# Recommendation ranker on one core: SyncE fetches one field of thirteen tiles, ScalarE another field of seven, GpSimd gathers 396 columns

## The chip, the core and the metric

The kernel runs on one core of a Trainium2 chip. TensorE (PE) multiplies, VectorE (DVE) and ScalarE (ACT) work on tiles in on-chip memory, GpSimd (POOL) issues the gathers from the embedding table, SyncE (SP) issues plain transfers. Each engine has its own instruction queue and waits on semaphores for the others. ScalarE has a queue of its own for issuing transfers, too: what stands in it is issued between its arithmetic instructions, in program order.

The metric is the device time of one execution in microseconds (us), as a median over runs.

## What is computed

A DCN ranker over 2048 rows of 26 ids. An id picks a 64-wide row of an embedding table; the 26 rows of an example make x0, 1664 wide.

```python
x0 = emb[ids].reshape(2048, 26 * 64)              # emb: 125000 x 64, float32
x = x0
for i in range(3):                                # cross layers
    x = x0 * (x @ cross_w[i])[:, None] + cross_b[i] + x
h = relu(x0 @ w1 + b1)                            # 1664 -> 1024
h = relu(h @ w2 + b2)                             # 1024 -> 512
h = relu(h @ w3 + b3)                             # 512 -> 256
y = sigmoid(concat([x, h], 1) @ out_w + out_b)
```

An id at or past the end of the table takes the table's last row.

## The kernel before

The 2048 rows are cut into 16 tiles (t = 0 to 15) of 128 rows, one row per partition. For each tile the 26 fields (f = 0 to 25) of 64 columns are brought into `x_buf[t % 2]`; two neighbouring fields make one chunk k of 128 columns, 13 chunks in all. The chunks go in four groups of 4, 3, 4 and 2 chunks (g = 0 to 3; fields 0 to 7, 8 to 13, 14 to 21, 22 to 25). In tile 15 the groups are cut finer and put in another order: chunks 0-3, 4-6, 7-8, 12, 9-10, 11 (`LAST_GROUPS`).

The way of a group through the engines, per tile: the fields land; DVE replaces rows of ids past the end (`make_whole`, line 516) and counts `x_whole`; PE transposes the chunks into a PSUM bank (`transpose_x`, line 729); ACT copies the bank to `xT_hi` (`x_hi`, line 400); DVE makes the remainder `xT_lo` (`x_lo`, line 523); PE multiplies by the first layer's weights in three passes (`l1`, line 717). After group 3 PE transposes the first layer's result (`transpose_h1`, line 771), once per tile, then runs the third layer of the tile before and the second layer of this tile inside the next tile's beginning. The order of each engine's queue is written out by hand (`begin`, `step`, `last_step`), tile after tile.

Most fields are brought by POOL: one indirect transfer gathers one field of one tile, 128 rows of 256 bytes (line 347). POOL goes through tiles and fields in order. In front of some fields it waits so as not to run too far ahead: at f = 16, from tile 2 on, for the transposition of group 0 of the same tile (line 320), among others.

The rest is fetched row by row, with one plain transfer of 256 bytes for each of 128 rows, whose table addresses come from `at_bytes`:

- SP fetches field `SP_FIELD` of the tiles in `SP_TILES` (lines 287 to 296). For a quarter of a tile it loads 32 addresses into registers (line 292) and issues 32 transfers (line 295), into one of four row buffers; from its fifth tile on it waits until the buffer has been emptied (line 289). SP has nothing else to do in that time.
- ACT fetches field `ACT_FIELD` of `ACT_TILES`, 64 rows per step in shares of 8, 12, 4, 16, 12 and 12 between its other work (`fetch`, line 377), into two row buffers. It does so in every step from tile 1 to tile 14.

In step t, right after `x_hi(t, 2)`, ACT copies the landed rows of SP's and of its own buffer into `x_buf` (`sp_place`, line 369; `act_place`, line 391), if the tile is in the list; `make_whole(t, 3)` waits for both. `of_pool` (line 67) tells which fields are left to POOL.

Of the kernel before, what the change touches and what calls it, by code (L numbers as in the profile page):

```python
# [5 lines left out]
def dcn_ranker_kernel(nc, r_ids, emb, cross_w, cross_b, w1, b1, w2, b2, w3, b3, out_w, out_b, out):  # L6
# [8 lines left out]
    B, F = r_ids.shape  # L15
# [4 lines left out]
    TILES = B // P  # L20
# [15 lines left out]
    def groups(t):  # L36
# [7 lines left out]
    LOW_BITS = 2 ** (H.bit_length() - 1) - 1  # L44

    SP_TILES = [2, 4, 6, 8, 9, 10, 12, 14, 15]
    SP_REGS = 32
    SP_FIELD = F - 2
    SP_BUFS = 4  # L50
# [2 lines left out]

    ACT_TILES = [3, 5, 7, 9, 11, 13, 15]
    ACT_FIELD = F - 1
    ACT_BUFS = 2
    ACT_SHARES = [8, 12, 4, 16, 12, 12]
    assert ACT_FIELD // FPK in GROUPS[-1] and all(
        sum(ACT_SHARES) * (t - 1) >= P * (j + 1) for j, t in enumerate(ACT_TILES)) and P % sum(ACT_SHARES) == 0  # L60
# [6 lines left out]
    def of_pool(t, f):  # L67
        return not (t in SP_TILES and f == SP_FIELD or t in ACT_TILES and f == ACT_FIELD)

# [37 lines left out]
    with ctx:  # L107
        def sb(name, shape, dt=F32):
            return ctx.enter_context(nc.sbuf_tensor(name, shape, dt))
# [4 lines left out]
        def sem(name):  # L114
            return ctx.enter_context(nc.semaphore(name))
# [32 lines left out]

        ONE_BY_ONE = len(SP_TILES) + len(ACT_TILES)
        assert (SP_BUFS + ACT_BUFS) * E + ONE_BY_ONE <= TILES * F  # L150
# [1 line left out]
        act_rows = [ids[:, (SP_BUFS + j) * E:(SP_BUFS + j + 1) * E].bitcast(F32) for j in range(ACT_BUFS)]  # L152
        sp_cols = ids[:, (SP_BUFS + ACT_BUFS) * E:(SP_BUFS + ACT_BUFS) * E + ONE_BY_ONE].bitcast(F32)
        at_bytes = sb("at_bytes", [ONE_BY_ONE, P], I32)
        at_row = {t: i for i, t in enumerate([t for t in SP_TILES if t % 2 == 0] + [t for t in SP_TILES if t % 2])}

        VR = (2 * CROSS + 1) * K1
        vec_rows = sb("vec_rows", [VR, P])
# [86 lines left out]
        sp_cols_ready = sem("sp_cols_ready")  # L245
# [31 lines left out]
        def _(sync):  # L277
# [8 lines left out]
            sync.wait_ge(sp_idx_ready, 1)  # L286
            for i, t in enumerate(SP_TILES):
                if i >= SP_BUFS:
# [61 lines left out]
        def _(act):  # L350
# [18 lines left out]
            def sp_place(t):  # L369
                i = SP_TILES.index(t)  # L370
                act.wait_ge(sp_landed[i % SP_BUFS], 16 * P * (i // SP_BUFS + 1))
                act.activation(x_buf[t % 2][:, SP_FIELD * E:(SP_FIELD + 1) * E], sp_rows[i % SP_BUFS],
                               ACT.Copy).then_inc(sp_placed, 1)
# [3 lines left out]
            def fetch(share):  # L377

                j, p = fetched[0] // P, fetched[0] % P
                if p == 0 and j >= ACT_BUFS:  # L380
                    act.wait_ge(act_placed, j - ACT_BUFS + 1)
                row = len(SP_TILES) + j
                regs = [act.alloc_register(f"act_row{j}_{p + i}") for i in range(share)]
# [7 lines left out]
            def act_place(t):  # L391
                j = ACT_TILES.index(t)
                act.wait_ge(act_landed[j % ACT_BUFS], 16 * P * (j // ACT_BUFS + 1))
                act.activation(x_buf[t % 2][:, ACT_FIELD * E:(ACT_FIELD + 1) * E], act_rows[j % ACT_BUFS],
                               ACT.Copy).then_inc(act_placed, 1)
# [90 lines left out]
        def _(dve):  # L486
# [8 lines left out]
            def split_lo(n):  # L495
                raw, _, lo = parts(n)
                for i in range(2):
                    dve.wait_ge(hi_staged, 2 * n + i + 1)
                    half = half_of(raw, i)
                    dve.tensor_tensor(half_of(lo, i), half, like(bank_of(n, i)[0], half),  # L500
                                      ALU.subtract).then_inc(weights_split, 1)

            def make_whole(t, g):
# [8 lines left out]
                if t in SP_TILES and SP_FIELD in range(a, a + n):  # L512
                    dve.wait_ge(sp_placed, SP_TILES.index(t) + 1)
                if t in ACT_TILES and ACT_FIELD in range(a, a + n):
                    dve.wait_ge(act_placed, ACT_TILES.index(t) + 1)
# [174 lines left out]
            link(dve.tensor_scalar(past[:, 0:QUICK], ids[:, 0:QUICK], float(H), None, ALU.is_ge))  # L690
            dve.wait_ge(idx_ready, 3)
            copied = 0
            for field, tiles in ((SP_FIELD, [t for t in SP_TILES if t % 2 == 0]), (SP_FIELD, [t for t in SP_TILES if t % 2]),
                                 (ACT_FIELD, ACT_TILES)):
                every = tiles[1] - tiles[0]
                assert tiles == list(range(tiles[0], tiles[-1] + 1, every))
                a, b = (t * F + field for t in (tiles[0], tiles[-1]))
                dve.scalar_tensor_tensor(out=sp_cols[:, copied:copied + len(tiles)], in0=past[:, a:b + 1:every * F], scalar=float(H),
                                         in1=idx[:, a:b + 1:every * F], op0=ALU.mult, op1=ALU.add).then_inc(sp_cols_ready, 1)
                copied += len(tiles)  # L700
# [11 lines left out]
        def _(pe):  # L712
# [195 lines left out]
            pe.transpose(h_bank[0][:, 0:VR], vec_rows[:, :], identity[0:VR, 0:VR]).then_inc(vecs_transposed, 1)  # L908
            pe.wait_ge(cross_ready, 1)

            pe.wait_ge(sp_cols_ready, 3)
            pe.transpose(x_bank[1][0:ONE_BY_ONE, 0:P], sp_cols, identity[:, :]).then_inc(sp_cols_transposed, 1)
            pe.wait_ge(sp_idx_ready, 1)
            pe.wait_ge(identity_r_set, 1)
# [30 lines left out]
```

## Time and profile before

| | |
|---|---|
| time, median of 3 runs | 529.95 us (529.79 to 530.59) |
| the profiled execution's own time | 530.56 us |
| its span (first to last instruction) | 528.8 us |
| PE busy in the span | 480.8 us (91%) |
| POOL busy in the span | 379.6 us (72%) |
| DVE, ACT busy | 186.4 us (35%), 84.7 us (16%) |
| granted TensorE clock | full (2.4 GHz) in all 40 slices |
| POOL gathers | 400, mean 0.947 us |
| single-row transfers of SP, of ACT | 1152 (9 tiles), 896 (7 tiles) |

The busy time of POOL counts the gathers only, not the 0.30 us between two of them, in which it is not free for anything else. Transfers that SP and ACT issue do not count as busy time of these engines. A tile lasts some 31 us; the first step, with the loading of the weights, ends near 53 us, and after tile 15's first layer near 516 us only the last layers are left.

### The profile page before, as it was taken

What the parts mean: (1) busy time and instruction counts of PE and PEld (TensorE: products, weight loads), DVE (VectorE), ACT (ScalarE), POOL (GpSimd) and SP (SyncE); (2) the same over time, 40 slices, a digit from 0 to 9 for tenths busy, and PEclk for the clock granted to TensorE, in tenths of its full rate; (3) what the DMA queues carried; (4) which work ended last, traced back from release to release, by engine and by line L of the source; (5) the groups of instructions that cost most, each with busy time, mean ns of one, the idle gap of its engine ahead of it and who ended that gap; (6) DMA issues with size and microseconds to landing.
All of it is one profiled execution on the core that took longest, in us unless ns stands there. A gap on an engine that the chain in (4) does not pass through costs nothing.

```text
span 528.8 us, 11324 instructions
## 1 busy us (share of the span) xinstructions
PE 480.8 (91%) x2912; PEld 442.2 (84%) x2912; DVE 186.4 (35%) x391; ACT 84.7 (16%) x159; POOL 379.6 (72%) x407
## 2 busy tenths in 40 slices
PE   2699899899999989899898989999899898999997
PEld 1399698898989889798887988888898888989996
DVE  5766414232142423224242321424232142423325
ACT  4642111111011111102011110101111010101111
POOL 5777776777777777777777777777777777777720
PEclk9999999999999999999999999999999999999999
DMA  7971111111111111111111111111111111111100
GB/s 234 387 263 29 28 29 27 28 29 27 29 29 29 28 28 30 29 29 29 27 29 26 30 27 30 26 30 29 26 30 25 30 27 28 27 28 28 28 10 2
DMA packets 19700, 24.90 MB, mean 47 GB/s; under 512 B 9305, under 2 KB 10292, under 8 KB 19636
## 3 DMA queue, kind: packets, MB, share of 16 engines
q0 software_dynamic: 12800, 13.13, 11.2%
q1 hardware_dynamic: 4770, 10.74, 5.7%
q10 hardware_dynamic: 2066, 0.31, 0.3%
q8 instruction: 23, 0.38, 0.3%
q14 instruction: 41, 0.34, 0.2%
HBM read 24.41 MB, written 0.01 MB: 46 GB/s over the span
## 4 chain that ended last, share of the span: by engine, by line
PE 55%; POOL 14%; issue 10%; ACTq 9%; DMA 5%; DVE 4%; ACT 3%; POOLq 0%; DVEq 0%
PE l_bank L717 41%; POOL x_raw L347 14%; ACTq L387 8%; DMA x_raw<-in_L_rec_emb,idx 4%; PE x_bank L717 4%; PE x_bank L729 4%; PE h_bank L771 3%; ACT xT_hi L400 2%; DVE x_raw L516 2%; ACTq L384 1%; PE l_bank L802 1%; DVE xT_lo L523 1%; PE h_bank L741 1%; DVE h2T_lo L528 1%; ACT h2T_hi L411 1%
## 5 line engine op out<-in xcount | busy, mean ns | idle before, releaser
L347 POOL DMA_INDIRECT x_raw<-in_L_rec_emb,idx x400 | 378.8, 947 | 125.5 <-issue 107.7
L717 PE MATMUL l_bank<-w_hi,xT_hi 128*128 128x342 f32 (+1 forms) x624 | 144.9, 333 | 3.5 <-DVE xT_lo L523 3.3
L717 PE MATMUL l_bank<-w_lo,xT_hi 128*128 128x342 f32 (+1 forms) x624 | 137.9, 321 | 0.0
L717 PE MATMUL l_bank<-w_hi,xT_lo 128*128 128x342 f32 (+1 forms) x624 | 137.7, 321 | 0.0
L717 PEld LDWEIGHTS l_bank<-w_hi,xT_hi 128*128 128x128 f32 x624 | 104.0, 191 | 7.9 <-DVE xT_lo L523 5.6
L717 PEld LDWEIGHTS l_bank<-w_lo,xT_hi 128*128 128x128 f32 x624 | 106.8, 191 | 0.0
L717 PEld LDWEIGHTS l_bank<-w_hi,xT_lo 128*128 128x128 f32 x624 | 106.3, 190 | 0.0
L523 DVE TENSOR_TENSOR xT_lo<-x_bank,xT_hi 128x512 fp32r<-128x512 f32 (+1 forms) x66 | 38.2, 578 | 158.5 <-ACT xT_hi L400 158.5
L400 ACT ACTIVATE xT_hi<-x_bank 128x512 fp32r<-128x512 f32 (+1 forms) x66 | 33.5, 507 | 270.3 <-PE x_bank L729 220.4
L729 PE MATMUL x_bank<-identity,x_raw 128*128 128x128 f32 x208 | 34.7, 279 | 27.0 <-DVE x_raw L516 27.0
L729 PEld LDWEIGHTS x_bank<-identity,x_raw 128*128 128x128 f32 x208 | 25.0, 142 | 36.7 <-issue 31.0
L516 DVE COPY_PREDICATED x_raw<-past,x_bank 128x512 f32<-128x512 int32 (+1 forms) x66 | 39.9, 605 | 42.7 <-DMA x_raw<-in_L_rec_emb,idx 42.7
L717 PE MATMUL l_bank<-w_hi,h1T_hi 128*128 128x512 f32 x120 | 48.7, 406 | 0.9 <-DVE h1T_lo L528 0.9
L717 PE MATMUL l_bank<-w_hi,h1T_lo 128*128 128x512 f32 x120 | 47.4, 395 | 0.0
L717 PE MATMUL l_bank<-w_lo,h1T_hi 128*128 128x512 f32 x120 | 47.2, 393 | 0.0
L535 DVE TENSOR_TENSOR h<-l_bank,b_rows 128x344 f32<-128x344 f32 (+2 forms) x48 | 23.2, 513 | 49.4 <-PE l_bank L717 49.4
L406 ACT ACTIVATE h1T_hi<-h_bank 128x512 fp32r<-128x512 f32 x30 | 17.6, 598 | 82.1 <-PE h_bank L771 82.1
L717 PEld LDWEIGHTS l_bank<-w_hi,h1T_lo 128*128 128x128 f32 x120 | 22.5, 188 | 5.3
L717 PEld LDWEIGHTS l_bank<-w_hi,h1T_hi 128*128 128x128 f32 x120 | 22.6, 188 | 5.0 <-DVE h1T_lo L528 1.1
L717 PEld LDWEIGHTS l_bank<-w_lo,h1T_hi 128*128 128x128 f32 x120 | 22.6, 189 | 4.1
L528 DVE SCALAR_TENSOR_TENSOR h2T_lo<-h_bank,h2T_hi 128x512 fp32r<-128x512 f32 (+1 forms) x16 | 10.8, 675 | 36.6 <-ACT h2T_hi L411 35.0
L528 DVE SCALAR_TENSOR_TENSOR h1T_lo<-h_bank,h1T_hi 128x512 fp32r<-128x512 f32 (+1 forms) x32 | 20.2, 670 | 9.8 <-ACT h1T_hi L406 9.7
(94 smaller groups left out, 296.5 us busy)
## 6 DMA issues: line engine op xcount, KB each, us to landing
ids<-in_L_rec_emb SPq DMA_DIRECT2D x1152, 0.2 KB
ids<-in_L_rec_emb ACTq DMA_DIRECT2D x896, 0.2 KB
w_raw<-in_L_rec_w SPq DMA_DIRECT2D x18, 512.0 KB, 15.0
x_raw<-in_L_rec_emb,idx POOLq DMA_INDIRECT x400, 2.4
b_rows<-in_L_rec_b SPq DMA_DIRECT2D x1, 512.0 KB
b_rows<-in_L_rec_b SPq DMA_DIRECT2D x1, 256.0 KB
ids<-in_r_ids SPq DMA_DIRECT2D x1, 208.0 KB, 2.7
b_rows<-in_L_rec_b SPq DMA_DIRECT2D x1, 128.0 KB
```

The source lines that it names most:

```text
L347: pool.indirect_dma_start(out=dst, out_offset=None, in_=emb, in_offset=rows).then_inc(landed, 16)
L384: act.load(regs, at_bytes[row:row + 1, p:p + share])
L387: act.dma_start(act_rows[j % ACT_BUFS][p + i:p + i + 1, :].bitcast(U8), emb_bytes[:, bass.DynSlice(at, ROW)], bounds_check="skip_entire_dm ...
L400: act.activation(xT_hi[:, ks[0]:ks[-1] + 1, :].rearrange("p k b -> p (k b)"), x_bank[g % 2][:, 0:len(ks) * P], ACT.Copy).then_inc(xT_hi_re ...
L406: act.activation(h1T_hi[:, half * HB:(half + 1) * HB, :].rearrange("p k b -> p (k b)"), h_bank[half][:, 0:HB * P], ACT.Relu).then_inc(h1T_ ...
L516: dve.copy_predicated(x_buf[t % 2][:, a * E:(a + n) * E].rearrange("p (f e) -> p f e", e=E), past[:, t * F + a:t * F + a + n].rearrange("p ...
L523: dve.tensor_tensor(xT_lo[:, ks[0]:ks[-1] + 1, :].rearrange("p k b -> p (k b)"), x_bank[g % 2][:, 0:len(ks) * P], xT_hi[:, ks[0]:ks[-1] + ...
L528: dve.scalar_tensor_tensor(out=lo, in0=bank[:, 0:cols], scalar=0.0, in1=hi.bitcast(F32), op0=ALU.max, op1=ALU.subtract).then_inc(done, 1)
L535: dve.tensor_tensor(h1[:, a:e], bank[:, 0:e - a], b1_rows[:, a:e], ALU.add).then_inc(h1_ready, 1)
L717: done = pe.matmul(bank[:, 0:b - a], x[:, k, :], w[:, k, a:b], start=(k == 0 and n == 0), stop=(k == last_k and n == 2))
L729: done = pe.transpose(x_bank[g % 2][:, i * P:(i + 1) * P], x_buf[t % 2][:, k * P:(k + 1) * P], identity[:, :])
L771: done = pe.transpose(bank[:, i * P:(i + 1) * P], h1[:, k * P:(k + 1) * P], identity[:, :])
```

## The change

Three numbers change. `SP_TILES` was nine tiles, `[2, 4, 6, 8, 9, 10, 12, 14, 15]`, and becomes the thirteen tiles 2 to 14; `SP_FIELD` stays 24. `ACT_FIELD` goes from 25 to 23, for the same seven odd tiles 3 to 15. POOL gathers what is left: 416 - 13 - 7 = 396 columns, where it was 400.

| tile | POOL's gathers before | after |
|---|---|---|
| 0, 1 | 26 | 26 |
| 2, 4, 6, 8, 10, 12, 14 | 25 | 25 |
| 3, 5, 7, 11, 13 | 25 | 24 |
| 9 | 24 | 24 |
| 15 | 24 | 25 |

The rest follows from that: since the tiles of SP are now one run with step 1, DVE picks SP's addresses in one instruction, not in two, and TensorE waits for two of them, not three.

```diff
-    SP_TILES = [2, 4, 6, 8, 9, 10, 12, 14, 15]
+    SP_TILES = list(range(2, TILES - 1))
...
-    ACT_FIELD = F - 1
+    ACT_FIELD = F - 3
...
-        at_row = {t: i for i, t in enumerate([t for t in SP_TILES if t % 2 == 0] + [t for t in SP_TILES if t % 2])}
+        at_row = {t: i for i, t in enumerate(SP_TILES)}
...
-            for field, tiles in ((SP_FIELD, [t for t in SP_TILES if t % 2 == 0]), (SP_FIELD, [t for t in SP_TILES if t % 2]),
-                                 (ACT_FIELD, ACT_TILES)):
+            for field, tiles in ((SP_FIELD, SP_TILES), (ACT_FIELD, ACT_TILES)):
...
-            pe.wait_ge(sp_cols_ready, 3)
+            pe.wait_ge(sp_cols_ready, 2)
```

POOL's queue at the end of tile 3, before: fields 20, 21, 22, then 23 and 24 in one row, then field 0 of tile 4.

```order
L347 DMA x_raw<-in_L_rec_emb,idx 128x64 [waits chunk_done]
L347 DMA x_raw<-in_L_rec_emb,idx 128x64
L347 DMA x_raw<-in_L_rec_emb,idx 128x64 [waits l2_done,chunk_done,x_transposed]
L347 DMA x_raw<-in_L_rec_emb,idx 128x64 x2
L347 DMA x_raw<-in_L_rec_emb,idx 128x64 [waits chunk_done,x_transposed]
```

The same place after: of fields 23, 24 and 25 only 25 is POOL's.

```order
L347 DMA x_raw<-in_L_rec_emb,idx 128x64 [waits chunk_done]
L347 DMA x_raw<-in_L_rec_emb,idx 128x64
L347 DMA x_raw<-in_L_rec_emb,idx 128x64 [waits l2_done,chunk_done,x_transposed]
L347 DMA x_raw<-in_L_rec_emb,idx 128x64
L347 DMA x_raw<-in_L_rec_emb,idx 128x64 [waits chunk_done,x_transposed]
```

One gather less stands between field 22 of an odd tile and the next tile's first.

DVE's queue in tile 15, groups 2 to 5 of `LAST_GROUPS`, before (`gathered_last` tells of POOL's landings, `act_placed` and `sp_placed` of ACT's copies):

```order
L516 COPY_PREDICATED x_raw<-past,x_bank 128x256 [waits gathered_last2]
L523 TENSOR_TENSOR xT_lo<-x_bank,xT_hi 128x256 [waits xT_hi_ready]
L516 COPY_PREDICATED x_raw<-past,x_bank 128x128 [waits act_placed,sp_placed]
L523 TENSOR_TENSOR xT_lo<-x_bank,xT_hi 128x128 [waits xT_hi_ready]
L516 COPY_PREDICATED x_raw<-past,x_bank 128x256 [waits gathered_last4]
L523 TENSOR_TENSOR xT_lo<-x_bank,xT_hi 128x256 [waits xT_hi_ready]
L516 COPY_PREDICATED x_raw<-past,x_bank 128x128 [waits gathered_last5]
```

And after:

```order
L516 COPY_PREDICATED x_raw<-past,x_bank 128x256 [waits gathered_last2]
L523 TENSOR_TENSOR xT_lo<-x_bank,xT_hi 128x256 [waits xT_hi_ready]
L516 COPY_PREDICATED x_raw<-past,x_bank 128x128 [waits gathered_last3]
L523 TENSOR_TENSOR xT_lo<-x_bank,xT_hi 128x128 [waits xT_hi_ready]
L516 COPY_PREDICATED x_raw<-past,x_bank 128x256 [waits gathered_last4]
L523 TENSOR_TENSOR xT_lo<-x_bank,xT_hi 128x256 [waits xT_hi_ready]
L516 COPY_PREDICATED x_raw<-past,x_bank 128x128 [waits act_placed,gathered_last5]
```

In the last tile chunk 12 (fields 24 and 25) comes from two POOL gathers now, which stand ahead of those of fields 18 to 21, and chunk 11 waits for ACT's copy as well.

## Rows read from the trace of the kernel before

**Rows 1.** Costliest groups: count, busy us, mean ns, idle us before them and its releaser

```profile
L347 POOL DMA_INDIRECT x_raw<-in_L_rec_emb,idx x400 | 378.8, 947 | 125.5 <-issue 107.7
L729 PE MATMUL x_bank<-identity,x_raw 128*128 128x128 f32 x208 | 34.7, 279 | 27.0 <-DVE x_raw L516 27.0
```

**Rows 2.** Chain that ended last (start us, us, what): `transpose_h1` of tiles 1, 2, 3, 5, 13, 14

```profile
84.05 1.15 PE h_bank L771 x8
114.71 1.15 PE h_bank L771 x8
145.24 1.15 PE h_bank L771 x8
...
206.37 1.15 PE h_bank L771 x8
...
455.35 1.15 PE h_bank L771 x8
486.04 1.15 PE h_bank L771 x8
```

**Rows 3.** Timeline (start us, us, what, idle before), tile 13: fields 20 and 21, `make_whole`, transposition of group 2

```profile
438.56 0.94 POOL L347 DMA_INDIRECT x_raw<-in_L_rec_emb,idx  x1 [0.30 <-issue]
439.81 0.94 POOL L347 DMA_INDIRECT x_raw<-in_L_rec_emb,idx  x1 [0.31 <-issue]
...
442.25 0.72 DVE L516 COPY_PREDICATED x_raw<-past,x_bank 128x512 f32<-128x512 int32 x1 [3.75 <-DMA x_raw<-in_L_rec_emb,idx]
...
443.12 0.63 PE L729 MATMUL x_bank<-identity,x_raw 128*128 128x128 f32 x4 [1.49 <-DVE x_raw L516]
```

**Rows 4.** Timeline, tile 3: ScalarE's share of 16 transfers, group 2 on ScalarE and TensorE

```profile
129.47 5.34 ACTq L387 DMA_DIRECT2D ids<-in_L_rec_emb  x16
134.86 0.60 ACT L400 ACTIVATE xT_hi<-x_bank 128x512 fp32r<-128x512 f32 x1 [6.19 <-issue]
...
132.22 0.60 PE L729 MATMUL x_bank<-identity,x_raw 128*128 128x128 f32 x4
...
136.24 0.58 PE L717 MATMUL l_bank<-w_hi,xT_hi 128*128 128x344 f32 x2 [0.58 <-DVE xT_lo L523]
```

**Rows 5.** Timeline, tile 2: group 0 transposed, POOL's field 16, group 2 transposed

```profile
89.23 0.60 PE L729 MATMUL x_bank<-identity,x_raw 128*128 128x128 f32 x4
...
90.63 0.94 POOL L347 DMA_INDIRECT x_raw<-in_L_rec_emb,idx  x1 [1.30 <-PE l_bank L717]
...
101.66 0.60 PE L729 MATMUL x_bank<-identity,x_raw 128*128 128x128 f32 x4
```

**Rows 6.** Timeline, tile 14: group 2 on ScalarE, placing of SP's rows, TensorE's next work

```profile
475.68 0.60 ACT L400 ACTIVATE xT_hi<-x_bank 128x512 fp32r<-128x512 f32 x1 [6.20 <-PE x_bank L729]
476.18 0.25 ACT L372 ACTIVATE x_raw<-ids 128x64 f32<-128x64 f32 x1
...
477.06 0.74 PE L717 MATMUL l_bank<-w_hi,xT_hi 128*128 128x344 f32 x3 [0.48 <-DVE xT_lo L523]
```

**Rows 7.** SP's register loads (ns min/median/max, first and last start), and its waits

```profile
L292 SPq TENSOR_LOAD <-at_bytes x36: 1869/2032/2190, 29.9 to 348.2; - x36
...
SPq L292 <- ACT x_raw L372: 27.9, 1, 27.9
```

**Rows 8.** POOL's gathers, 100 to 260 us, then 360 to 470 us: ns, and landing min/median/max

```profile
L347 POOL DMA_INDIRECT x_raw<-in_L_rec_emb,idx x129: 940/944/1098, 99.4 to 259.3; - x129
...
DMA to landing us min/median/max: 2.3/2.4/3.6
...
L347 POOL DMA_INDIRECT x_raw<-in_L_rec_emb,idx x89: 940/944/1159, 359.5 to 470.0; - x89
...
DMA to landing us min/median/max: 2.3/2.4/3.3
```

**Rows 9.** Timeline, tile 15: POOL's field 18, `make_whole` of chunks 9 and 10

```profile
498.70 0.95 POOL L347 DMA_INDIRECT x_raw<-in_L_rec_emb,idx  x1 [0.30 <-issue]
...
507.68 0.43 DVE L516 COPY_PREDICATED x_raw<-past,x_bank 128x256 f32<-128x256 int32 x1
```

## The prediction

> **What bounds the kernel now.** I read the groups first, then the chain of waits by tile, then the timeline inside single tiles. The groups show one engine that is never free and one that waits for it: POOL's 400 gathers take 378.8 us and the gaps in front of them 125.5 us, together 504.3 us or 1.26 us a gather, and TensorE stands idle 27.0 us in front of the transpositions of x, released by VectorE's `make_whole` [rows 1]. Between two gathers lies 0.30 us although nothing that the profile shows is waited for: a gather starts every 1.25 us [rows 3]. So a tile of 25 gathers costs POOL 31.25 us and one of 24 costs 30.00 us.
>
> The chain gives TensorE's own pace. The marks of `transpose_h1` are 30.66 us apart from tile 1 to 2, 30.53 us from tile 2 to 3, and (206.37 - 84.05) / 4 = 30.58 us on average from tile 1 to 5; from tile 5 to 13 it is (455.35 - 206.37) / 8 = 31.12 us [rows 2]. POOL begins with a lead, loses 31.25 - 30.58 = 0.67 us of it per tile, and is the bound once the lead is used up.
>
> Tile 13 shows what that looks like: field 21's gather starts at 439.81, VectorE's `make_whole` follows at 442.25, released by the landing, and TensorE transposes group 2 at 443.12 after 1.49 us of idleness [rows 3]. So group 2 is transposed 3.31 us after field 21's gather starts, when POOL decides. In tile 3 the same transposition, at 132.22, waited for nothing; there TensorE waits a little later, 0.58 us, for `xT_lo`, because ACT could not copy group 2 before its 16 row transfers (5.34 us) were issued [rows 4]. This ACT wait is hidden in tiles where POOL makes TensorE wait earlier. It will be back when POOL stops doing so: the whole 1.49 us is not to be had.
>
> **What the change removes.** Four gathers fewer in all, but what counts is how many fewer stand ahead of a given place. Ahead of field 21 of tile 13, SP had seven tiles of field 24 and ACT five of field 25 before; now SP has eleven (2 to 12) and ACT five of field 23: four gathers, 4 x 1.25 = 5.00 us. POOL alone would let tile 13's group 2 be transposed at 443.12 - 5.00 = 438.12, and the mark of tile 13 would come at 438.12 + (455.35 - 443.12) = 450.35 [rows 2, 3].
>
> TensorE's own pace gives 206.37 + 8 x 30.58 = 451.01 for the same mark [rows 2]. That is the later of the two, so TensorE with ACT's waits becomes the bound, and POOL ends 0.66 us ahead of it: the gain at tile 13 is 455.35 - 451.01 = **4.34 us**, not 5.00. The two stay close all the way, since a pair of tiles is 49 gathers, 61.25 us, against 61.16 us.
>
> Bounds of that term: with 30.53 us a tile the mark is at 450.61 and the gain 4.74 us; with 30.66 us it is 451.65 and 3.70 us [rows 2]. I take the mean, since four tiles stand in it.
>
> **Does POOL's gate give it back?** With a lead POOL can run into its wait at field 16 for group 0 of the same tile. In tile 2 it did: group 0 was transposed at 89.23, field 16 started at 90.63 after 1.30 us of idleness, 1.00 more than usual [rows 5]. (The row names L717, whose matmuls count up another semaphore of the same wait; the program's line 320 waits for the transposition.) But the gate only holds POOL 1.40 us behind group 0, and from there tile 2's fields went through without a wait: field 21 started 5 gathers later, at 96.88, plus 3.31 gives 100.19, and TensorE came at 101.66, so 1.47 us was left [rows 3, 5]. A tile of 25 gathers takes 0.67 us of that and the next of 24 gives 0.58 us back. A stall at the gate costs nothing, then, as long as it leaves these 1.47 us.
>
> **Tile 14, tile 15 and the end: nothing.** In tile 14 ACT copies group 2 at 475.68 at the end of its share of 16, and TensorE waits for it at 477.06 [rows 6]; an earlier POOL does not move that. From tile 14's mark at 486.04 to the end of the span at 528.8 TensorE's work follows on itself [rows 2]. Tile 15 has one gather more, and fields 24 and 25 stand ahead of 18 to 21. Field 18 started at 498.70; five fewer before tile 15 and two more in it make three fewer ahead of it, 494.95. Field 21 starts 3.75 later and lands 2.4 after its start [rows 8], at 501.1; `make_whole` takes it at 507.68 - 4.34 = 503.34 [rows 9]. That leaves 2.2 us: hidden.
>
> **What SP and ACT pay.** SP issues 512 more row transfers and loads 16 more times. Its 36 loads run from 29.9 to 348.2 us with one wait of 27.9 us, so a quarter of a tile takes (348.2 - 29.9 - 27.9) / 35 = 8.30 us, and a tile 33.2 us [rows 7]. That is slower than a tile of the loop, and SP has no pause left: 52 quarters end at 29.9 + 52 x 8.30 = 461.5. How long a single row takes to land no row tells; the nearest are the gathers, 2.3 to 3.6 us, and I take their median of 2.4 [rows 8]: 463.9. Tile 14's rows are placed at 476.18 - 4.34 = 471.84 [rows 6]. **Eight us remain**, the smallest margin, and it hides SP's work. The four buffers hold it back nowhere, since SP falls behind, not ahead. On ACT an odd tile now has two placings, 0.25 us each [rows 6], in front of the share of 12 and so of group 3's copy. Five odd tiles (3, 5, 7, 11, 13) have one more than before: between 0 and 5 x 0.25 = 1.25 us. I take 0, because the wait that TensorE has on ACT in tile 3 is for group 2, whose copy comes before the placing [rows 4]. DVE's and TensorE's address set-up is one instruction shorter, once, beside weight loading: nothing.
>
> Do SP's transfers slow the others when they never pause? In 100 to 260 us, when SP issues nearly all the time, a gather takes 944 ns and lands in 2.4 us; in 360 to 470 us, when SP is through, it is 944 ns and 2.4 us; the slowest landings are 3.6 and 3.3 us [rows 8]. I take zero, with 0.3 us as the upper end.
>
> The Trainium skill speaks against the change at this point: "DMA: Bandwidth & Descriptors", section "Issuing engines are not separate DMA queues", says that transfers of all issuing engines share the same 16 DMA engines, and that issuing from several saves only the sequencer's issue time, usually small. By it the four gathers would only be elsewhere and the sum near zero. Here the trace disagrees with "small": issue is what POOL runs out of.
>
> **Sum.** 530.56 - 4.34 = 526.2 us for the profiled execution (span 524.5); it lay 0.61 us above the median of 529.95, so the median goes to **525.6 us**.
>
> **Rivals.** (a) *SP comes late; slower.* ACT's queue then stands in front of tile 14's placing, and with it the copies of groups 3 and the next tile. The first wait comes when a quarter takes over (471.84 - 2.4 - 29.9) / 52 = 8.45 us; the time is 0.2% worse than before when the rows come 5.4 us after 471.84, at 8.56 us a quarter, 3.1% over what SP shows. At that point the time is 529.95 + 1.06 = 531.0 us. Against it: the 8.30 is a mean over 35 quarters. For it: the margin is only eight us after 440, and SP runs without pause for the first time. 4%.
>
> (b) *Transfers share; no change.* As a mechanism of this kernel: landings grow longer with SP always at work, and group 2 is later by that. Since POOL has 0.66 us in hand at tile 13, a landing longer by 0.66 + 4.34 = 5.0 us would give the whole gain back, once and not per tile: 529.9 us. That is the skill's rule above as a rival; rows 8 speak against it. 4%.
>
> (c) *POOL stays the bound.* Gate stalls or late landings take 1 to 3 us more of POOL's lead than tile 2 shows; the mark of tile 13 then follows POOL and 1.5 to 3.5 us are gained: 526.5 to 528.5, say 527.5. For it: POOL and TensorE are within 0.66 us at tile 13. 10%.
>
> (d) *ACT's wait does not come back.* Then POOL's 5.00 us are gained and a little more at tile 14: 524.5 us. Against it: tiles 2 and 3 show the ACT wait wherever POOL doesn't wait. 4%.
>
> (e) That the change doesn't do what it says is excluded by the queues: four gathers fewer and 512 row transfers more stand there.
>
> **How the numbers follow.** The forecast has 78%, its own range 525.0 to 526.4 (gains of 4.74 and 3.70, with a little for the spread of the runs, 529.79 to 530.59). The range for 8 in 10 takes in (d) and half of (c): 524.6 to 527.4. About 0.2%, 1.06 us, is what a measurement here can tell from no change. Faster: forecast, (c) and (d), 92%; same 4%; slower 4%.
>
> **What the profile after should show.** 396 gathers, still 1.25 us apart. TensorE's idle time in front of x's transpositions falls from 27.0 us by some 10 (the waits of tiles 5 to 14 like tile 13's go); waits for `xT_lo` near 0.6 us appear in tiles 4 to 13; marks 30.6 us apart through tile 13. SP's 52 loads end near 460 us with no wait for a buffer. I would be wrong if marks past tile 5 stay at 31 us or more, if a placing on ACT waits for SP's landing, or if SP's quarters grow past 8.4 us.

## The result, and the profile after

The changed kernel takes 522.93 us (median of 4 runs, 522.64 to 523.27), the kernel before in the same comparison 529.87 us (529.25 to 530.59): the ratio is 0.9869, with a 95% interval of 0.9852 to 0.9886. That is 6.9 us faster, where 4.3 us were forecast; the time lies 1.7 us below the lower end of the range, 524.6 us. The profiled execution after took 522.85 us with a span of 521.1 us, 7.7 us shorter than the span before.

Two groups of the profile after answer to [rows 1]; the third is TensorE's matmuls of the first layer. (Lines past 690 have moved up by one: 716 is 717 of before, 728 is 729, 770 is 771. PEld are TensorE's weight loads; ACTq and SPq are the queues in which ScalarE and SyncE issue transfers.)

```profile
L347 POOL DMA_INDIRECT x_raw<-in_L_rec_emb,idx x396 | 375.5, 948 | 123.2 <-issue 106.7
L728 PE MATMUL x_bank<-identity,x_raw 128*128 128x128 f32 x208 | 34.7, 279 | 22.7 <-DVE x_raw L516 22.7
L716 PE MATMUL l_bank<-w_hi,xT_hi 128*128 128x342 f32 (+1 forms) x624 | 144.8, 333 | 0.0
```

A gather still costs (375.5 + 123.2) / 396 = 1.26 us. The third line is the surprise: TensorE's idle time in front of the first layer's matmuls, which the forecast said would come back as a wait for `xT_lo`, is 0.0 us. Before, there were six such waits (us in total, times, longest):

```profile
PE l_bank L717 <- DVE xT_lo L523: 3.3, 6, 0.7
```

TensorE's matmuls no longer wait for ScalarE in any tile.

The chain of waits of after (start us, us, what) gives the marks of `transpose_h1` for the tiles 1, 2, 3, 5, 13 and 14, to be held against [rows 2]:

```profile
82.03 1.15 PE h_bank L770 x8
111.35 1.15 PE h_bank L770 x8
144.17 1.15 PE h_bank L770 x8
...
203.78 1.15 PE h_bank L770 x8
...
449.47 1.15 PE h_bank L770 x8
478.39 1.15 PE h_bank L770 x8
```

Tile 2 lasts 29.32 us (30.66 before), tile 14 lasts 28.92 us (30.69 before): TensorE's own pace is no longer 30.58 us a tile. In tile 2 two waits account for most of that: the one for `xT_lo`, 0.61 us before, is gone, and the one in front of group 1's transposition is 0.57 us, where it was 1.16 us. First tile 2 of before, then of after:

```profile
97.05 0.52 PE L729 MATMUL x_bank<-identity,x_raw 128*128 128x128 f32 x3 [1.16 <-DVE x_raw L516]
105.71 0.74 PE L717 MATMUL l_bank<-w_hi,xT_hi 128*128 128x344 f32 x3 [0.61 <-DVE xT_lo L523]
```

```profile
94.46 0.52 PE L728 MATMUL x_bank<-identity,x_raw 128*128 128x128 f32 x3 [0.57 <-DVE x_raw L516]
```

Between tile 3 and tile 13 the marks are (449.47 - 144.17) / 10 = 30.53 us apart. That is about POOL's pace: a tile has 24.5 gathers on average there, 24.5 x 1.25 = 30.6 us. The mark of tile 13 comes 5.88 us earlier than before, that of tile 14 7.65 us earlier; nothing is lost or won after that.

In tile 13 (timeline: start us, us, engine, what, idle before) the same three instructions as in [rows 3]:

```profile
433.99 0.95 POOL L347 DMA_INDIRECT x_raw<-in_L_rec_emb,idx  x1 [0.32 <-issue]
...
436.38 0.72 DVE L516 COPY_PREDICATED x_raw<-past,x_bank 128x512 f32<-128x512 int32 x1 [4.19 <-DMA x_raw<-in_L_rec_emb,idx]
...
437.25 0.63 PE L728 MATMUL x_bank<-identity,x_raw 128*128 128x128 f32 x4 [1.93 <-DVE x_raw L516]
```

TensorE waits 1.93 us for POOL here, more than the 1.49 us before. POOL is still the bound, with fewer gathers, and TensorE needs less time for a tile than it did.

And this is ScalarE in tile 3 of after (timeline), to be held against [rows 4]:

```profile
124.33 0.49 ACT L400 ACTIVATE xT_hi<-x_bank 128x384 fp32r<-128x384 f32 x1 [1.92 <-PE x_bank L728]
125.47 3.49 ACTq L387 DMA_DIRECT2D ids<-in_L_rec_emb  x16
131.11 0.60 ACT L400 ACTIVATE xT_hi<-x_bank 128x512 fp32r<-128x512 f32 x1 [6.29 <-PE x_bank L728]
131.61 0.25 ACT L372 ACTIVATE x_raw<-ids 128x64 f32<-128x64 f32 x1
131.75 0.24 ACT L394 ACTIVATE x_raw<-ids 128x64 f32<-128x64 f32 x1
```

The share of 16 takes 3.49 us, where it took 5.34 us, and ScalarE then waits for TensorE, not the other way round. The program issues the same number of transfers of the same size. What differs is the field, and with it the ids. The durations of ScalarE's transfers (line 387; ns min/median/max) before, then after, and of SP's (line 295) before:

```profile
L387 ACTq DMA_DIRECT2D ids<-in_L_rec_emb x896: 234/235/532, 55.4 to 486.7; - x180
```

```profile
L387 ACTq DMA_DIRECT2D ids<-in_L_rec_emb x896: 90/90/516, 55.1 to 477.2; - x180
```

```profile
L295 SPq DMA_DIRECT2D ids<-in_L_rec_emb x1152: 42/73/318, 32.1 to 356.4; - x192
```

### The profile page after: what moved, and what is told of

It is laid out like the page before. It is cut to its first block, busy times and chain, and to the rows that moved or that the text cites. A ratio compares the mean times of both kernels' runs of the same rounds, so it can differ in the third digit from the quotient of the medians.

```text
span 521.1 us, 12362 instructions
## 1 busy us (share of the span) xinstructions
PE 481.6 (92%) x2912; PEld 445.0 (85%) x2912; DVE 186.3 (36%) x390; ACT 85.4 (16%) x163; POOL 376.4 (72%) x403
## 4 chain that ended last, share of the span: by engine, by line
PE 70%; POOL 11%; issue 7%; DMA 6%; DVE 4%; ACT 1%; POOLq 0%; DVEq 0%
PE l_bank L716 55%; POOL x_raw L347 11%; DMA x_raw<-in_L_rec_emb,idx 5%; PE x_bank L728 5%; PE x_bank L716 4%; PE h_bank L770 3%; DVE x_raw L516 2%; PE l_bank L801 1%; DVE h2T_lo L528 1%; ACT h2T_hi L411 1%; PE h_bank L740 1%; PE h_bank L812 1%; DMA ids<-in_r_ids 1%; PE l_bank L740 0%; PE h_bank L716 0%
## 5 line engine op out<-in xcount | busy, mean ns | idle before, releaser
L347 POOL DMA_INDIRECT x_raw<-in_L_rec_emb,idx x396 | 375.5, 948 | 123.2 <-issue 106.7
L716 PE MATMUL l_bank<-w_hi,xT_lo 128*128 128x342 f32 (+1 forms) x624 | 139.2, 324 | 0.0
L716 PEld LDWEIGHTS l_bank<-w_hi,xT_lo 128*128 128x128 f32 x624 | 107.8, 192 | 0.0
L716 PEld LDWEIGHTS l_bank<-w_hi,xT_hi 128*128 128x128 f32 x624 | 105.3, 192 | 2.6 <-DVE xT_lo L523 0.3
L770 PE MATMUL h_bank<-identity,h 128*128 128x128 f32 x124 | 20.6, 287 | 0.8 <-DVE h L535 0.8
```

The costliest lines, as they stand in the source:

```text
L347: pool.indirect_dma_start(out=dst, out_offset=None, in_=emb, in_offset=rows).then_inc(landed, 16)
L716: done = pe.matmul(bank[:, 0:b - a], x[:, k, :], w[:, k, a:b], start=(k == 0 and n == 0), stop=(k == last_k and n == 2))
L770: done = pe.transpose(bank[:, i * P:(i + 1) * P], h1[:, k * P:(k + 1) * P], identity[:, :])
```

## Experiments: is it the skipped rows?

**SP's part alone.** ScalarE back on field 25, nothing else.

```diff
-    ACT_FIELD = F - 3
+    ACT_FIELD = F - 1
```

> The changed kernel with ScalarE back on field 25: SP's part of the change alone. In the inputs all 2048 ids of field 25 lie inside the table, but only 259 of field 23 and 248 of field 24; a row transfer whose address lies past the table is skipped (skip_entire_dma). Theory A (skipped rows): with field 25 ScalarE's 896 transfers are all carried out, at 0.34 us each, its shares stay long, TensorE waits 0.6 us per tile for xT_lo, and the recorded forecast holds: 525.6 us (525.0 to 526.4), marks of transpose_h1 30.6 us apart. Rival B (the forecast had POOL's or the gate's size wrong and the field that ScalarE fetches has no part): the same as the changed kernel, 522.9 us.

Measured: 526.26 us against 530.42, ratio 0.9914 (0.9897 to 0.993), single runs from 524.95 to 527.5. Three of the six lie near 525.2 us and three near 527.3 us; what separates them is open, and the profile is that of the longest. The median lies in Theory A's range, and no run comes near rival B's 522.9 us. The timeline of its tile 3 has the long share and the wait for `xT_lo` again, as in [rows 4]:

```profile
128.95 5.37 ACTq L387 DMA_DIRECT2D ids<-in_L_rec_emb  x16
134.37 0.60 ACT L400 ACTIVATE xT_hi<-x_bank 128x512 fp32r<-128x512 f32 x1 [6.22 <-issue]
...
135.75 0.74 PE L716 MATMUL l_bank<-w_hi,xT_hi 128*128 128x344 f32 x3 [0.59 <-DVE xT_lo L523]
```

Its waits (us in total, times, longest) show that this is so in every step from 1 to 14:

```profile
PE l_bank L716 <- DVE xT_lo L523: 10.5, 14, 2.0
```

**The same field 23, but no row skipped.** ScalarE's addresses for ids past the end point at a row inside the table; `make_whole` replaces the row as before.

```diff
-            for field, tiles in ((SP_FIELD, SP_TILES), (ACT_FIELD, ACT_TILES)):
+            for field, tiles, beyond in ((SP_FIELD, SP_TILES, float(H)), (ACT_FIELD, ACT_TILES, 0.0)):
...
-                dve.scalar_tensor_tensor(out=sp_cols[:, copied:copied + len(tiles)], in0=past[:, a:b + 1:every * F], scalar=float(H),
+                dve.scalar_tensor_tensor(out=sp_cols[:, copied:copied + len(tiles)], in0=past[:, a:b + 1:every * F], scalar=beyond,
```

> The changed kernel, but ScalarE's addresses for ids past the end point at a row inside the table (the row is replaced afterwards as before), so that none of its 896 transfers is skipped; field, tiles and order are those of the changed kernel. Theory A: ScalarE's shares are as long as with field 25 and the time goes back to 525.6 us (525.0 to 526.4). Rival C (it is the place of field 23 in its group, or the order of the last tile, that helps): stays at 522.9 us.

Measured: 526.51 us against 530.42, ratio 0.9926 (0.991 to 0.9941). That is 0.1 us above Theory A's range, and the single runs spread as widely as with field 25, from 525.33 to 527.38. This kernel differs from the changed kernel by one constant. Its transfers take as long as field 25's:

```profile
L387 ACTq DMA_DIRECT2D ids<-in_L_rec_emb x896: 234/235/517, 54.4 to 482.6; - x180
```

This settles the cause: rival C falls, and the skipping is worth 526.51 - 523.2 = 3.3 us, give or take the spread of 1 us (523.2 is the changed kernel timed again, below). Rows that are carried out also load the DMA engines, but POOL's gathers do not show it: from 100 to 260 us they take 947 ns and land in 2.4 us here, 944 ns and 2.4 us in the changed kernel. What ScalarE's queue takes for a row is what counts.

**The same for SP.** The constants the other way round: none of SP's rows is skipped.

```diff
-            for field, tiles in ((SP_FIELD, SP_TILES), (ACT_FIELD, ACT_TILES)):
+            for field, tiles, beyond in ((SP_FIELD, SP_TILES, 0.0), (ACT_FIELD, ACT_TILES, float(H))):
```

> The changed kernel, but SP's addresses for ids past the end point inside the table, so that none of SP's 1664 transfers is skipped. Theory A: a row that is carried out costs SP about 0.34 us in place of 0.17 to 0.19, so a tile takes 128 x 0.335 + 4 x 2.03 = 51 us, longer than the loop's 30.5: SP's rows come late from the first tiles on, tile 14's at 30 + 13 x 51 = 693 us, and with the 51 us that follow its placing the kernel takes about 745 us. Rival B (a row costs SP the same, skipped or not): 522.9 us.

Measured, in one run: 745.86 us, where Theory A had 745. SP's transfers take 228 ns, ScalarE waits for SP's landings at twelve of the thirteen placings, and TensorE waits for ScalarE's placings in turn:

```profile
L295 SPq DMA_DIRECT2D ids<-in_L_rec_emb x1664: 227/228/323, 31.6 to 692.0; - x185
```

```profile
ACT x_raw L372 <- DMA ids<-in_L_rec_emb: 257.3, 12, 24.3
```

So rival (a) of the prediction, SP coming late, is a real mechanism with this price. It rests on the data: the eight microseconds that the forecast found are there because seven in eight of SP's rows are skipped.

**ScalarE's part alone.** The kernel before, with field 23.

```diff
-    ACT_FIELD = F - 1
+    ACT_FIELD = F - 3
```

> The kernel before with ScalarE on field 23, POOL still at 400 gathers: ScalarE's part alone. Theory A: TensorE runs through tiles 1 and 2 in 29 us each, POOL no longer stalls at its gate in tile 2 (1.0 us) and tile 14 no longer waits for ScalarE (1.8 us), while POOL at 25 gathers a tile sets the pace between: 529.9 - 2.8 = 527.1 us (526.5 to 527.6). Rival B: no effect, 529.9 us.

Measured: 529.77 us against 530.42, ratio 0.9986 (0.9978 to 0.9995): 0.65 us faster, where 2.8 us were expected. The expectation fell. It added the gains at the gate and in tile 14 as if POOL were not there. In the timeline TensorE waits 1.38 us for POOL in tile 14, and then goes on without a wait for `xT_lo`:

```profile
474.38 0.63 PE L729 MATMUL x_bank<-identity,x_raw 128*128 128x128 f32 x4 [1.38 <-DVE x_raw L516]
...
476.43 0.74 PE L717 MATMUL l_bank<-w_hi,xT_hi 128*128 128x344 f32 x3
```

Before, that last row came at 477.06 [rows 6]: 0.63 us, and that is the whole gain. With 400 gathers POOL decides, and a faster ScalarE is of almost no use. SP's part alone gives 530.42 - 526.26 = 4.2 us, ScalarE's alone 0.65 us, both together 6.9 us: more than the sum. Each bound lies just behind the other, so a gain on one is cut short by the other.

## Experiments: is POOL the bound now, and can it be moved?

**The changed kernel again**, on the chip of the three that follow.

> The changed kernel itself, on the same chip as the three below, to compare with: 523 us.

Measured: 523.2 us (523.12 to 523.44) against 530.35, ratio 0.9863 (0.9849 to 0.9878).

**One gather more.** SP leaves tile 2's field to POOL.

```diff
-    SP_TILES = list(range(2, TILES - 1))
+    SP_TILES = list(range(3, TILES - 1))
```

> The changed kernel with SP on the tiles 3 to 14 only: POOL gathers one field more, in tile 2. Theory A (once ScalarE's rows are skipped, POOL decides from tile 3 to tile 13): one gather is one gather, 1.25 us more than the changed kernel, 524.2 us. Rival D (TensorE or ScalarE decides in part of these tiles): less than half of that, 523.0 to 523.5 us.

Measured: 524.59 us, 1.4 us more than the changed kernel beside it. Theory A holds and rival D falls: one gather more costs its 1.25 us in full. So POOL decides from tile 3 to tile 13.

**Gathers taken from POOL.** If ScalarE's rows are cheap, ScalarE can fetch more of them. Two kernels raise its shares from 64 rows a step to 80 and to 96, and give it more tiles; a share is split where a tile's 128 rows end. The diff is that of 96 rows; with 80 the shares are 10, 14, 6, 16, 20 and 14.

```diff
-    ACT_TILES = [3, 5, 7, 9, 11, 13, 15]
+    ACT_RUNS = [[3, 7, 11, 15], [4, 8, 12], [5, 9, 13]]
+    ACT_TILES = sorted(sum(ACT_RUNS, []))
...
-    ACT_SHARES = [8, 12, 4, 16, 12, 12]
+    ACT_SHARES = [16, 14, 8, 16, 24, 18]
...
+                rest = max(0, p + share - P)
+                share -= rest
...
+                if rest:
+                    fetch(rest)
```

> The changed kernel with ScalarE fetching 80 rows of field 23 per step instead of 64, for the tiles 3, 5, 6, 8, 10, 11, 13 and 15: one gather fewer for POOL ahead of field 21 of tile 13. Theory A: 1.25 us less than the changed kernel, 521.7 us. Rival D: no gain, 523 us.

> The changed kernel with ScalarE fetching 96 rows of field 23 per step, for the tiles 3, 4, 5, 7, 8, 9, 11, 12, 13 and 15: three gathers fewer for POOL ahead of field 21 of tile 13. Theory A: 3 x 1.25 = 3.75 us less than the changed kernel, 519.2 us, as long as ScalarE's longer shares stay off TensorE's path; what is left then is TensorE's own 29.2 us a tile. Rival E (the longer shares put ScalarE's wait back): 521 to 524 us, with waits for xT_lo in the rows.

Measured: 587.81 us (ratio 1.1082) and 641.5 us (ratio 1.2108). Far slower than any of the theories had it. The waits for `xT_lo` that rival E named are there, but with 96 rows they come to 70.7 us in 27 waits. The timeline of the 96-row kernel in tile 6 shows where (in these kernels line 408 is 400 of above, 390 is 384, the loading of addresses, 393 is 387 and 736 is 728): after the copy that starts at 264.69 ScalarE's queue issues the next transfer only at 268.66, 3.97 us later. In the changed kernel above, 16 transfers follow 1.14 us after the start of the same copy, at 125.47.

```profile
264.69 0.49 ACT L408 ACTIVATE xT_hi<-x_bank 128x384 fp32r<-128x384 f32 x1 [3.79 <-issue]
268.66 3.21 ACTq L393 DMA_DIRECT2D ids<-in_L_rec_emb  x16
271.91 0.60 ACT L408 ACTIVATE xT_hi<-x_bank 128x512 fp32r<-128x512 f32 x1 [6.73 <-issue]
272.41 0.25 ACT L374 ACTIVATE x_raw<-ids 128x64 f32<-128x64 f32 x1
277.54 0.45 ACTq L393 DMA_DIRECT2D ids<-in_L_rec_emb  x3
```

In between lies the load of 16 addresses into registers. Shares that are no multiple of four words had moved the starts of many loads to 8 bytes past a multiple of 16. Two more kernels have shares that are all multiples of four words.

```diff
-    ACT_SHARES = [16, 14, 8, 16, 24, 18]
+    ACT_SHARES = [16, 16, 8, 16, 24, 16]
```

> As the kernel with 96 rows per step, but with shares of 16, 16, 8, 16, 24 and 16, so that every load of addresses into ScalarE's registers starts at a multiple of four 4-byte words. In the rows of the kernels with 80 and 96 rows, loads that start elsewhere take 3.3 to 5.5 us, against 0.5 to 1.7 us from a multiple of four. Theory F (the start of the loads made those two kernels slow): the loads are short, POOL decides again, and three gathers fewer give 523.2 - 3.75 = 519.4 us, up to 521 us if the share of 24 makes TensorE wait. Rival G (96 rows are too many for ScalarE's queue whatever their start): over 530 us.

Measured: **519.18 us** (518.81 to 519.37) against 530.17, ratio 0.9791 (0.9778 to 0.9805). Theory F holds, rival G falls. The loads (ns min/median/max) of the slow 96-row kernel, then of this one:

```profile
L390 ACTq TENSOR_LOAD <-at_bytes x87: 513/2002/5522, 53.6 to 578.5; - x87
```

```profile
L390 ACTq TENSOR_LOAD <-at_bytes x83: 560/1217/1727, 53.5 to 452.1; - x83
```

The expectation read the slow rows too broadly: in them, too, a load of 2 words from such a start takes 0.5 to 0.8 us and one of 8 words 1.8 to 2.1 us; the long loads are slow. This is the fastest kernel of the study, 4.0 us below the changed kernel (3.8 us if each is held against the kernel before on its own chip), with three gathers fewer ahead of tile 13's field 21 (3 x 1.25 = 3.75). Its wait for POOL in tile 13 has shrunk to 0.28 us, from 1.93:

```profile
433.50 0.63 PE L736 MATMUL x_bank<-identity,x_raw 128*128 128x128 f32 x4 [0.28 <-DVE x_raw L524]
```

For 80 rows the shares became 12, 16, 4, 16, 20 and 12.

> As the kernel with 80 rows per step, with shares of 12, 16, 4, 16, 20 and 12: the same start of the loads as before the change, at multiples of four words. Theory F: one gather fewer than the changed kernel, 523.2 - 1.25 = 522.0 us. Rival G: over 525 us.

Measured: 523.35 us (522.09 to 523.9) against 530.17, ratio 0.9866 (0.985 to 0.9882): over 60 us better than with the other starts, but no better than the changed kernel, where 1.25 us were expected. In the profiled execution the gather does count up to tile 13: group 2 is transposed at 436.38, 1.40 us before the changed kernel's 437.78 in its second profile. Right after, the granted clock falls. A view by stretches shows it from 436.4 to 440.0 us and then to 450.0 us (length; busy us and instructions of PE, PEld, DVE, ACT, POOL; granted clock as a share of 2.4 GHz; DMA share; GB/s).

```profile
436.40:440.00 3.60, 3.60 (x15) 3.60 (x16) 1.04 (x2) 0.89 (x3) 2.69 (x4) 0.55 0.14 26
440.00:450.00 10.00, 10.00 (x65) 9.97 (x65) 1.21 (x3) 0.39 (x1) 7.56 (x9) 0.99 0.16 29
```

TensorE loses the gain there, and tile 14 has no wait for POOL left in which it could be made up: its group 2 is transposed at 467.86, against 467.91. The other three executions have mean granted clocks of 0.993, 0.996 and 0.997, so the clock fell in them too, but they were not profiled, and where it fell isn't shown. One of them took 522.09 us, what was expected. So the fallen clock explains the profiled execution; for the median it is a guess.

## Why the prediction was wrong, point by point

- **The bound before, and a gather's price: right.** 1.25 us a gather, POOL running out of its lead, TensorE waiting for group 2. One gather more costs 1.4 us.
- **What the change removes: right, but the other side of the comparison was wrong.** Four gathers are 5.00 us at tile 13. The step that failed is "TensorE's own pace gives 206.37 + 8 x 30.58 = 451.01 for the same mark". 30.58 us is the pace with ScalarE on field 25. The prediction listed what ScalarE pays as one more placing and passed over the field number, although that was one of the three changed numbers: it took a row transfer to cost the same whatever its id. After, TensorE alone takes 29.3 us for tile 2, POOL comes later than that, and POOL's removed time counts in full. With ScalarE's rows not skipped, 526.26 and 526.51 us are measured, near the forecast of 525.6 us.
- **The gate: right that it takes nothing, wrong that it gives nothing.** POOL's field 16 of tile 2 starts at 89.56 without the extra 1.00 us of [rows 5], since TensorE is some 2 us earlier by then (group 0 is transposed at 87.22, before at 89.23). At tile 13 the gain is 5.88 us: 5.00 from the gathers and 1.00 from the gate, less 0.12 that no row accounts for. The prediction also set the row's releaser aside wrongly. The wait of line 320 was through at 89.91 (first row below, of before); the gather itself then waited for `chunk_done` (line 340), which a second-layer matmul of L717 counted up at its end, 90.52 (second row).

```profile
L320 POOLq EVENT_SEMAPHORE  x1: 43/43/43, 89.9 to 89.9; - x1
```

```profile
90.13 0.39 PE L717 MATMUL l_bank<-w_hi,h1T_lo 128*128 128x512 f32 x1
```

- **Tile 14: "nothing" was wrong.** [rows 6] showed that ScalarE's share of 16 decided there. That share takes 3.33 us after. But TensorE had waited for POOL in the same tile, too, 1.27 us (row below, of before). After, both waits are gone: 1.27 + 0.48 = 1.75 us, and tile 14 is 30.69 - 28.92 = 1.77 us shorter. It took both parts of the change. With ScalarE on field 23 alone, POOL makes TensorE wait 1.38 us there; with SP's part alone, the wait for `xT_lo` in that tile is 2.0 us. 5.88 + 1.77 = 7.65 of the 7.7 us of span.

```profile
474.52 0.63 PE L729 MATMUL x_bank<-identity,x_raw 128*128 128x128 f32 x4 [1.27 <-DVE x_raw L516]
```

- **SP: right on its pace, for a reason that the prediction did not see.** 52 loads from 28.8 to 452.2 us make (452.2 - 28.8 - 1.4) / 51 = 8.27 us a quarter, as against 8.30; the 1.4 us is one wait for a buffer, where none was forecast. No placing waits for SP. But the pace holds only as long as the rows are skipped.
- **Transfers sharing the engines: right that it costs nothing.** From 100 to 260 us of after a gather takes 944 ns and lands in 2.4 us, 3.4 at the slowest. The rule of the Trainium skill that the prediction set against the change ("DMA: Bandwidth & Descriptors", section "Issuing engines are not separate DMA queues") has issue time as usually small relative to the transfer itself. This case does not agree: a gather holds POOL for 1.25 us of the 2.4 us to its landing, and issue time decided, by 1.25 us a gather on POOL and 145 ns a row on ScalarE's queue.
- **The rivals.** (d), ScalarE's wait not coming back, is what happened; it had 4%, and its 524.5 us left out the gate and most of tile 14. The evidence held against it, the waits of tiles 2 and 3, was evidence on field 25. (c) had it right that POOL stays the bound, with 10%, but looked for the reason in a slower POOL; it was a TensorE that no longer waits for ScalarE, and the time went the other way.
- **The signs of being wrong: none came.** The marks are 30.53 us apart, no placing waits for SP's landing, SP's quarters take 8.27 us. That the marks came out as forecast is luck: 30.6 was meant as TensorE's pace and is POOL's. What did tell was a sign of being right that stayed away, the waits for `xT_lo` in tiles 4 to 13.

```profile
L372 ACT ACTIVATE x_raw<-ids x9: 247/248/249, 104.8 to 505.9; 128x64 f32<-128x64 f32 x9
```

The placings, of which this row of before tells (line 372, ns), cost nothing, as the prediction took it: five odd tiles have one more of 248 ns, and ScalarE has time for it. In tile 3 of after it waits for TensorE again until 138.53, before its copy of group 3.

## What to carry to other kernels

When a change swaps which data an instruction works on, count and shape being equal, ask whether its cost depends on the data: here two rows of one trace, 73 ns for one engine's transfers and 235 ns for another's of the same form, would have been the hint. A floor that is read from the trace ("this engine's own pace") is valid only as long as nothing in the change touches what makes it. And two bounds within 2% of each other are not added up: each part alone gave 4.2 and 0.65 us, both gave 6.9.

## What the runs showed of the hardware

- A row transfer that the bounds check skips still takes its place in the issuing queue, but (medians) 90 ns instead of 235 ns on ScalarE's and 73 ns instead of 228 ns on SP's.
- A long load of addresses into ScalarE's registers that starts 8 bytes past a multiple of 16 bytes is slow. In the trace of the first 96-row kernel, 16 words took 3.5 to 3.9 us from such a start (13 loads) and 1.2 to 1.4 us from a multiple of 16 (14 loads). There 24 words took 5.4 to 5.5 us, and 1.7 us from a multiple of 16 in the second 96-row kernel. Other starts were not tried.
- After a wait of TensorE of 1.9 to 2.0 us the granted clock falls, in some cases, to the lower level (1.2 GHz) for 3.4 us. In the changed kernel's first profile it did so in tiles 3 and 9, and not in tiles 7 and 13 after waits of 1.99 and 1.93 us; in its second profile, with four such waits, nowhere. The time is nearly the same (522.85 and 523.44 us), because TensorE then waits the less for POOL: in front of group 2 of tiles 4 and 5, no wait and 1.01 us in the first profile, 0.77 and 1.96 us in the second, and likewise in tiles 10 and 11. The clock in 40 slices (tenths of full speed), first and second profile:

```profile
PEclk9999999999899999999999998999999999999999
```

```profile
PEclk9999999999999999999999999999999999999999
```
